# Cross-attention loop: the inverse of the softmax sums by logarithm, exponential and Newton step, with a new order of the steps on each engine

## The reference, cut to what matters

```python
h = _layernorm(x)
qh = split(h @ wq + bq); kh = split(ctx @ wk + bk); vh = split(ctx @ wv + bv)
logits = einsum('bhqd,bhkd->bhqk', qh, kh) / sqrt(16)      # then the mask
attn = softmax(logits, axis=-1)
x = x + merge(einsum('bhqk,bhkd->bhqd', attn, vh)) @ wo + bo
```

## Time and profile before

| | us |
|---|---|
| median of 3 runs | 1198.31 (1197.46 to 1198.68) |
| the profiled execution, its own time | 1199.42 |
| its span in the profile | 1197.7 |
| busy in the span: PE, PEld | 1024.8, 795.3 |
| busy in the span: DVE, ACT, POOL | 855.8, 560.2, 491.8 |

### The profile page before, as it was taken

One profiled execution on the slowest core, in us unless ns is written; L12 is line 12 of the kernel. 1 busy time (PEld: TensorE's weight loads), 2 busy tenths in 40 slices (PEclk: granted clock), 3 DMA queues, 4 the chain that ended last, 5 costly groups with the idle time before them and its releaser, 6 DMA issues. The chain is left out here.

```text
span 1197.7 us, 24813 instructions
## 1 busy us (share of the span) xinstructions
PE 1024.8 (86%) x9211; PEld 795.3 (66%) x9226; DVE 855.8 (71%) x1867; ACT 560.2 (47%) x1104; POOL 491.8 (41%) x494
## 2 busy tenths in 40 slices
PE   0779999999479999999999977999999967888886
PEld 0657776777368888888888865777777743444443
DVE  0747777777666666676676575777777756888886
ACT  0245555555343333333333244555555535777775
POOL 0134444444213322332233322444444427999991
PEclk9969999999779999999999997999999987999999
DMA  9300000000000000000000040000000000000000
GB/s 322 60 1 2 2 2 2 2 2 2 1 1 1 0 0 0 0 0 0 0 0 0 1 137 1 2 2 2 2 2 2 2 1 1 23 24 25 23 23 27
DMA packets 19420, 20.97 MB, mean 18 GB/s; under 512 B 6528, under 2 KB 17920, under 8 KB 19072
## 3 DMA queue, kind: packets, MB, share of 16 engines
q1 hardware_dynamic: 17712, 19.12, 5.2%
q10 hardware_dynamic: 1616, 0.58, 0.3%
HBM read 15.51 MB, written 4.19 MB: 16 GB/s over the span
## 5 line engine op out<-in xcount | busy, mean ns | idle before, releaser
L398 POOL TENSOR_TENSOR sm_a<-sm_a,mx_a 128x616 f32<-128x616 f32 x128 | 153.2, 1218 | 282.2 <-DVE mx_a L565 282.2
L666 POOL TENSOR_TENSOR hl_f<-hf_f,hh_f 128x512 fp32r<-128x512 f32 x80 | 103.6, 1295 | 262.4 <-ACT hh_f L790 262.4
L530 ACT ACTIVATE pt_a<-pT_a 128x512 f32<-128x512 f32 (+1 forms) x192 | 101.0, 528 | 175.7 <-PE pT_a L453 175.5
L558 DVE TENSOR_TENSOR sm_a<-pS_a,mask 128x616 f32<-128x616 f32 x128 | 101.1, 791 | 43.8 <-PE pS_a L439 43.8
L689 PE MATMUL pGU_f<-xh_f,wgh_f 128*128 (+1 forms) x320 | 128.7, 402 | 0.0
L785 ACT ACTIVATE sg_f<-pGU_f 128x512 f32<-128x512 f32 x80 | 47.9, 599 | 170.1 <-PE pGU_f L691 170.0
L691 PE MATMUL pGU_f<-xh_f,wgl_f 128*128 (+1 forms) x320 | 125.3, 392 | 0.0
L690 PE MATMUL pGU_f<-xl_f,wgh_f 128*128 (+1 forms) x320 | 125.3, 392 | 0.0
L896 DVE TENSOR_TENSOR hf_f<-pGU_f,sg_f 128x512 f32<-128x512 f32 x80 | 55.4, 692 | 90.7 <-ACT sg_f L785 90.7
L906 DVE SCALAR_TENSOR_TENSOR x<-pD_f,coef_f,x 128x256 f32 (+1 forms) x256 | 106.2, 477 | 18.3 <-PE pD_f L728 16.8
L570 DVE RECIPROCAL rc_a<-pO_a 128x256 f32<-128x256 f32 x64 | 111.9, 1748 | 8.6 <-PE pO_a L467 8.6
(11 more groups left out here) (182 smaller groups left out, 2273.8 us busy)
## 6 DMA issues: line engine op xcount, KB each, us to landing
x<-x_in SPq DMA_DIRECT2D x4, 1024.0 KB, 14.0
out_x<-x SPq DMA_DIRECT2D x32, 128.0 KB, 1.7
gu<-gu_in SPq DMA_DIRECT2D x1, 2560.0 KB, 15.5
aw<-aw_in SPq DMA_DIRECT2D x2, 1024.0 KB, 11.6
w<-w_in SPq DMA_DIRECT2D x2, 1024.0 KB, 6.5
dn<-dn_in SPq DMA_DIRECT2D x1, 1280.0 KB, 14.6
b<-b_in SPq DMA_DIRECT2D x1, 512.0 KB, 9.4
g<-g_in SPq DMA_DIRECT2D x1, 512.0 KB, 10.2
```

The source lines that it names most:

```text
L398: pool.tensor_tensor(heads, heads, mx[u][:, g, :].rearrange("p (h a) -> p h a", a=1).broadcast_to([P, HG, SK]), ALU.subtract).then_inc(shi ...
L530: act.activation(pt[u][:, lo:lo + n, :].rearrange("p n t -> p (n t)"), pT[:, (J * t + j) % 2, 0:n * P], ACT.Copy).then_inc(pt_sb, 1)
L558: dve.tensor_tensor(sm[u][:, g, :].rearrange("p (b h k) -> p b h k", b=2, k=SK), pS[:, 2 * g:2 * g + 2, 0:HS].rearrange("p b (h k) -> p b ...
L666: pool.tensor_tensor(hl[u][:], hf[u][:], f32(hh[u][:]), ALU.subtract).then_inc(hl_ok, 1)
```

## The change

What it does, in the attention phase of both layers:

- The inverse of the sums is no longer a DVE reciprocal. ACT `inverse` computes exp(-ln(sum)) with two activations over 128x256, DVE `refine` makes one Newton step with two operations (through a new tile rf), leaving the inverse with its sign changed, and `normalise` multiplies with a factor -1.
- `q_out` moves from ACT (two activations) to DVE (one operation over 128x256, with the bias broadcast).
- The order of the steps is new. PE makes the scores of tile t+2 before it projects tile t-1, and transposes x one tile earlier (t+3) and behind the projection. ACT begins with the inverse and ends with xt_out(t+3) and norm(t+4). DVE does both maxima, then q_out, the refining and the product, one mask, and only then the add. The lead is 4 instead of 3.

```diff
@@ tensor
             def step(t, u, has):
                 if has(0):
                     turn_p(t, u, 0)
-                if has(2):
-                    turn_x(t + 2, u)
-                if has(0):
                     turn_p(t, u, 1)
                 if has(2):
                     queries(t + 2, u)
                 if has(0):
                     turn_p(t, u, 2)
+                if has(2):
+                    scores(t + 2, u)
                 if has(-1):
                     project(t - 1, 1 - u)
-                if has(2):
-                    scores(t + 2, u)
+                if has(3):
+                    turn_x(t + 3, 1 - u)
                 if has(0):
                     weigh(t, u)
 
-            lay_out_steps(step, 3, 1)
+            lay_out_steps(step, 4, 1)
@@ scalar
-            def q_out(t, u):
-                act.wait_ge(q_ps, t + 1)
-                count(act, scored, G * (t - 1))
-                for g in range(G):
-                    last = act.activation(q[u][:, g * P:(g + 1) * P], pA[:, D + g * P:D + (g + 1) * P], ACT.Identity,
-                                          bias=bqkv[:, 0, g:g + 1])
-                last.then_inc(q_sb, 1)
...
+            def inverse(t, u):
+                act.wait_ge(weighed, t + 1)
+                act.activation(rc[u][:], pO[:, D:2 * D], ACT.Ln).then_inc(logged, 1)
+                act.wait_ge(logged, t + 1)
+                act.activation(rc[u][:], rc[u][:], ACT.Exp, scale=-1.0).then_inc(recips, 1)
+
             def step(t, u, has):
+                if has(-1):
+                    inverse(t - 1, 1 - u)
                 if has(0):
                     pt_out(t, u, 0)
-                if has(2):
-                    xt_out(t + 2, u)
-                if has(0):
                     pt_out(t, u, 1)
-                if has(2):
-                    q_out(t + 2, u)
-                if has(0):
                     pt_out(t, u, 2)
                 if has(1):
                     exp(t + 1, 1 - u, 0)
                     exp(t + 1, 1 - u, 1)
                 if has(3):
-                    norm(t + 3, 1 - u)
+                    xt_out(t + 3, 1 - u)
+                if has(4):
+                    norm(t + 4, u)
@@ vector
+            def q_out(t, u):
+                dve.wait_ge(q_ps, t + 1)
+                count(dve, scored, G * (t - 1))
+                dve.tensor_tensor(q[u][:].rearrange("p (g n) -> p g n", g=G),
+                                  pA[:, D:2 * D].rearrange("p (g n) -> p g n", g=G),
+                                  bqkv[:, 0, :].rearrange("p (g a) -> p g a", a=1).broadcast_to([P, G, P]),
+                                  ALU.add).then_inc(q_sb, 1)
+
+            def refine(t, u):
+                dve.wait_ge(recips, t + 1)
+                dve.tensor_tensor(rf[:], pO[:, D:2 * D], rc[u][:], ALU.mult).then_inc(refined, 1)
+                dve.wait_ge(refined, 2 * t + 1)
+                dve.scalar_tensor_tensor(rc[u][:], rf[:], -2.0, rc[u][:], ALU.add, ALU.mult).then_inc(refined, 1)
+
             def normalise(t, u):
-                dve.wait_ge(weighed, t + 1)
-                dve.reciprocal(rc[u][:], pO[:, D:2 * D]).then_inc(recips, 1)
                 count(dve, projected, t - 1)
-                dve.wait_ge(recips, t + 1)
-                dve.tensor_tensor(ot[u][:], pO[:, 0:D], rc[u][:], ALU.mult).then_inc(o_norm, 1)
+                dve.wait_ge(refined, 2 * t + 2)
+                dve.scalar_tensor_tensor(ot[u][:], pO[:, 0:D], -1.0, rc[u][:], ALU.mult, ALU.mult).then_inc(o_norm, 1)
...
                     largest(t + 1, 1 - u, 1)
+                if has(2):
+                    q_out(t + 2, u)
                 if has(-1):
+                    refine(t - 1, 1 - u)
                     normalise(t - 1, 1 - u)
-                    add(t - 1)
                 if has(2):
                     mask(t + 2, u, 0)
                 if has(-1):
+                    add(t - 1)
                     stats(t - 1, 1 - u)
```

More of the change, by code:

```diff
@@ L363, in attention_phase @@
         pst = lambda n, s, d=F32: ctx.enter_context(nc.psum_tensor(n + tag, s, d))
-        (padded, normed, xt_ps, xt_sb, q_ps, q_sb, scored, masked, maxed, shifted, exped, pt_ps, pt_sb,
+        (padded, logged, refined, normed, xt_ps, xt_sb, q_ps, q_sb, scored, masked, maxed, shifted, exped, pt_ps, pt_sb,
          weighed, recips, o_norm, projected, biased, added, stated) = (sem(n) for n in (
-             "padded", "normed", "xt_ps", "xt_sb", "q_ps", "q_sb", "scored", "masked", "maxed", "shifted",
+             "padded", "logged", "refined", "normed", "xt_ps", "xt_sb", "q_ps", "q_sb", "scored", "masked", "maxed", "shifted",
              "exped", "pt_ps", "pt_sb", "weighed", "recips", "o_norm", "projected", "biased", "added", "stated"))
@@ L373, in attention_phase @@
         xn, xt, q, ot, rc = (pair(n, [P, D]) for n in ("xn", "xt", "q", "ot", "rc"))
+        rf = sbt("rf", [P, D])
         sm = pair("sm", [P, G, NS])
```

## The result

| | before | changed |
|---|---|---|
| median | 1197.92 us (4 runs) | 1236.2 us (4 runs, 1233.36 to 1237.15) |
| ratio | | 1.0315, 95% interval 1.0297 to 1.0333 |
| span of the profiled execution | 1197.7 | 1235.4 |

The change makes the kernel 3.2% slower. The forecast was 1231, its range 1210 to 1265.

The account below looks back on a forecast made before the run. No engine was full; a loop through VectorE's 1.75 us reciprocal set 7.45 us per tile. The new period of 7.90 adds 26.1 us over 58 tiles, the drains 6.2: +32.3, forecast 1231 us, range 1210 to 1265.

Parts of the forecast that it names:

- the sum: Whole kernel: 58 steady tiles at 0.45 us give 26.1, drains 6.2, fill nothing; total +32.3 us.
- the drain: Last tiles of each layer, where nothing hides the longer inverse: 3.1 us more per layer, 6.2 in all.
- Two loads per tile: ScalarE in the attention phase: a table load before the logarithm and one before the inverse's exponential, 128 in all.
- Rival A: ScalarE's inverse: one set serves both functions, no loads in the loop; period 7.35 to 7.45, about 1194 us; chance 0.08.
- The price of a load: ScalarE, between two activations: 1.30 us from the end of one to the start of the next.
- rival C: ScalarE's busy queue: a table switch costs twice its row; period 10.5 us, about 1388 us; chance 0.02.
- Rival B: Load ahead of the logarithm is held by the logarithm's wait; period 9.16 us, about 1311 us; chance 0.03.
- The loop: Steady tile through weighing, inverse, probability copies, third transposes, scores, projection and add: period 7.86 us.
- The second loop: ScalarE from projection through transpose and copy of x, normalisation and load to the logarithm: 7.90 us, nearly equal to 7.86.
- ScalarE's busy share: Sign in the attention stage: ScalarE's busy share rises from 53% to about 83%.
- Rival D: TensorE's clock falls as the loop idles more; a quarter of tiles at the lower level, about 1300 us; chance 0.03.
- VectorE: Per tile: 1.35 us added for refining and q_out against 1.75 removed, about 0.4 us shorter, over 2 us slack.

Follow-up runs that it names:

- the run with one set: Changed kernel with one table set holding logarithm and exponential loaded once at the start of each attention phase: 1204.57 us, 1.006 of the kernel before.
- the stretch taken away: Changed kernel with one table set loaded per attention phase, and GpSimd's bias addition also waiting for the previous tile's projection: 1196.97 us, 0.9987 of the kernel before.
- the run without the first load: Changed kernel with a copy in place of the logarithm and a logarithm in place of the inverse's exponential: 1231.96 us, 1.0285 of the kernel before.
- the best kernel here: Changed kernel reordered so TensorE makes queries of tile t+3 between projection and weighing, with VectorE's reciprocal: 1145.38 us, 0.9565 of the kernel before.
- inverse alone, with loads: Kernel before, its order and q_out kept, reciprocal replaced by logarithm, exponential and refining, table sets chosen by the build: 1282.99 us, 1.0694 of before.
- queries early: Changed kernel with one table set and the new inverse, reordered so TensorE makes queries of tile t+3 before the weighing: 1160.26 us, 0.9685 of before.
- the run of the inverse alone with one set: Kernel before, its order and q_out kept, reciprocal replaced by logarithm, exponential and refining, one table set per attention phase: 1176.76 us, 0.9831 of before.

## Why the prediction was right

The prediction was right in its mechanism: the load between the two activations holds back the copies of the probabilities, and TensorE waits for them. One term of the sum, the drain, was mis-sized.

**Two loads per tile** were forecast from the row at 45.76, a load for one function only. The profile shows 128, half in front of each activation. The Trainium skill (ScalarE: Activation LUTs, Table sets: the hidden batching unit) is right that one set holds both functions, as the run with one set shows; its rule that a logarithm followed by an exponential costs one load did not hold for a kernel that leaves the choice to the build. Rival A, the same mechanism with the loads gone, was put at 7.35 to 7.45; the run gave 7.54 and, with the stretch taken away, 7.35.

**The price of a load**, 1.30 us from the end of one activation to the start of the next: 161.77 - 0.02 to 163.06 is 1.31. The further 1.38 us that the Trainium skill gives for a switch (ScalarE: Activation LUTs, What ACT_TABLE_LOAD costs) is not seen between any of the 64 pairs of logarithm and exponential, and rival C fell with that. Rival B fell with the row at 159.97: the load runs before the logarithm's wait is over.

**The loop** came out nearly step by step, from the first transposes on (forecast, then measured): exponential's end 2.25, 2.25; third transposes 2.82, 2.79; scores 3.12, 3.15; projection 4.36, 4.39; add 5.51, 5.56; weighing 5.98, 6.04; period 7.86, 7.92. q_out stood at 2.1 and came at 2.02. The second loop, through ScalarE, was forecast as the one that binds with 7.90; it does not, the run without the first load shows the period unchanged. Both were 0.04 apart in the working, so the sum did not feel it. ScalarE's busy share came to 87% of the stretch, where 83% was forecast.

**The sum.** Forecast 26.1 us for the steady tiles and 6.2 for the two drains. From the second tile's first transposes to those of the tile before last, 29 steps, the changed kernel takes 230.09 and 230.10 us in the two layers (81.71 to 311.80, 767.27 to 997.37), the one before 215.78 and 215.39: 29.0 together. From there to the last statistics of the layer it is 24.63 and 24.43 against 19.03 and 18.77: 11.3. The sum of 40.3, less 2.4 us by which the changed kernel's first attention layer had reached its second tile earlier (1.8 of it before its first normalisation), leaves 37.9, and the spans differ by 37.7. The 2.4 us are luck: the forecast took nothing for the start, and no run shows that they belong to the change (the first normalisation starts anywhere from 61.6 to 64.1 us in the eleven profiles). The term that was mis-sized is **the drain**, 5.6 us per layer and not 3.1. I had priced the longer inverse alone; what it brings with it is TensorE's clock:

```profile
315.81 2.07 PE L476 MATMUL pO_a<-aw,ot_a 128*128 128x256 f32 x4 [0.78 <-DVE ot_a L581]
...
318.40 0.66 PE L468 MATMUL pO_a<-pt_a,V 128*32 128x128 f32 x8 [0.52 <-DVE x L586]
```

After a wait of 1.70 us and one of 0.78 the projection takes 2.07 us instead of 1.13 and eight matmuls of the weighing 0.66 instead of 0.43: TensorE is at the lower of its two levels, 1.2 GHz, in part of this stretch (granted clock 0.71 from 311 to 322 us). Each stretch of a drain (projection to add, weighing to the next transposes or to the last inverse) can be set against the same stretch at full clock. By that the lower level costs 4.0 and 3.8 us in the changed kernel's two drains and 1.7 and 1.4 us in those of the kernel before. The difference, 2.3 us per layer, leaves 3.3 us for the longer inverse, close to the 3.1 forecast.

In the run without the first load the drain of the first layer took 20.7 us (313.13 to 333.84), 3.9 less than in the changed kernel. By the same reckoning 2.6 us of this are the clock, since half a weighing and part of one projection ran at the lower level. The other 1.3 us are a load that is missing: no softmax exponential stands between the last two inverses of a layer, so the last one finds its set (62 loads ahead of the second activation instead of 64). In the second layer that load is missing too, but 4.9 us went to the clock, and the drain took 24.3. The clock also makes part of the spread between runs of one kernel: with the bias addition moved, the three runs at a mean granted clock of 0.958 took 1193 us, and the seven at 0.952 to 0.955 took 1195 to 1198. Rival D was thus real, but only in the drains.

**VectorE** was forecast 0.4 us shorter per tile. The windows show 42.42 us of 60 at 7.92, 5.60 per tile, against 46.95 at 7.44, 5.82: 0.2 shorter, the rest being the stretched operation. It was on no path there.

## What to carry to other kernels

Before an activation function is added to a loop, look in the profile at which functions stand beside it and count the table loads that it will bring; choose the set by hand if one holds all of them. A load costs nothing where its engine waits anyway. Where another engine waits for what is queued behind it, it costs what that engine cannot fill with other work (here 0.38 us of 1.3 in one order and nearly all of it in the other), so its place matters more than its number. Look for something else that the waiting engine can do before a slow operation (here a 1.75 us reciprocal) is replaced: covered in that way, it gave the best kernel here. And count, for every operation that is added, what it will run beside.

## What the hardware showed that I had not expected

**VectorE beside GpSimd.** The second refining operation has both tensors in SBUF. It takes 0.42 us with GpSimd's bias addition moved away, 0.61 us where 0.33 us of the two overlap, 0.84 us beside the end of the subtractions and the start of the addition, and 1.00 us where the 0.72 us addition lies wholly inside it (171.01, above); the first refining operation, with one tensor in PSUM, took 0.41 to 0.43 us throughout. The Trainium skill (VectorE: DVE Perf Modes, Two Vector instructions with no wait between them) mentions a second SBUF read interface shared with GpSimd and used by operations with two SBUF tensors; that fits these rows. The price is not fixed, but the rows show what sets it: the operation ends 0.28 us after the GpSimd operation that runs when it starts, or starts with it. So it ends at 169.72 behind an addition that ends at 169.44 (one set), at 172.01 behind 171.73 (inverse alone, with loads), and at 169.96 behind 169.68 (queries early). The same 0.28 to 0.29 us stands at all 414 meetings in the eight profiles that have the refining. In the run of the inverse alone with one set the operation starts at 171.14 beside a subtraction that ends at 171.29, ends at 171.57, and so keeps its 0.43 us. GpSimd pays in its turn: its operation that starts behind the meeting takes 0.18 us more, there the next subtraction (1.40 instead of 1.22, both together 2.57 instead of 2.39), and with the queries early the addition (0.91 instead of 0.73).

**The clock in a steady loop.** In the run of the inverse alone with loads TensorE waits 1.75 us in one piece in every tile. In six of its steady tiles the period is 10.0 to 10.2 us instead of 8.52. One of them, with the next for comparison:

```profile
232.21 2.02 PE L476 MATMUL pO_a<-aw,ot_a 128*128 128x256 f32 x4
234.16 2.06 PE L440 MATMUL pS_a<-K,q_a 64*128 64x308 f32 x8
...
242.30 1.05 PE L476 MATMUL pO_a<-aw,ot_a 128*128 128x256 f32 x4
243.28 1.31 PE L440 MATMUL pS_a<-K,q_a 64*128 64x308 f32 x8
```

Projection and scores take 0.97 and 0.75 us more, and the granted clock of 180 to 240 us is 0.97 where it was 1.00 from 120 to 180: TensorE is at 1.2 GHz in part of that tile, 1.3 us after a wait of 1.75 us. The tiles at full clock have the same wait. Nothing in the rows tells why these six fell and the others did not. The changed kernel, with waits of 0.80 and 0.30 us, shows no such tile.
